# Attention to a context of 77 tokens: f16 pairs, a column of ones and a six-step order

## The reference

```python
q = split_heads(queries @ Wq + bq)          # 2 x 16 x 1024 x 16
k = split_heads(keys @ Wk + bk)             # 2 x 16 x 77 x 16, from ctx_1024
v = split_heads(values @ Wv + bv)
scores = jnp.einsum('bhqd,bhkd->bhqk', q, k) / jnp.sqrt(jnp.float32(HD))
scores = jnp.where(mask, -1e15, scores)     # layer 2
# layer 3: scores + attn_bias (2 x 16 x 1024 x 77), then where(mask == 0, -inf, scores)
attn = jax.nn.softmax(scores, axis=-1)
out = (attn @ v, heads side by side) @ Wo + bo
```

## Time and profile before

| what | value |
|---|---|
| runs, us | 3884.24, 3891.68, 3892.88 (median 3891.68) |
| profiled execution, us | 3897.72 |
| its span in the trace, us | 3896.1 |
| mean granted TensorE clock | 0.871 of 2.4 GHz |
| instructions | 66000 |
| block `c2a` in the trace | 2391.7 to 2544.0 us |
| block `c3a` in the trace | 3371.5 to 3526.8 us |

### The profile page before, as it was taken

How to read it: one execution, slowest core, us unless ns; L and a number is a source line. 1 busy time by engine, 2 the same in 40 slices (tenths; PEclk the granted TensorE clock), 3 DMA queues, 4 the chain that set the end, 5 groups by cost and what they waited for, 6 DMA issues and landing times. The chain is left out here.

```text
span 3896.1 us, 66000 instructions
## 1 busy us (share of the span) xinstructions
PE 3167.6 (81%) x24836; PEld 2157.7 (55%) x24837; DVE 2087.9 (54%) x3105; ACT 1832.3 (47%) x2854; POOL 1173.6 (30%) x851
## 2 busy tenths in 40 slices
PE   4979995816879998889994986968999999794495
PEld 2756664304436665346663654854666666583364
DVE  2968885493568763567853224635444444363122
ACT  2448883341348882358861112425555565242131
POOL 1239994000027880058761011210000000151102
PEclk7669997957889998989996996968999999796698
DMA  2421110000012210022216011001100000235211
GB/s 66 164 75 55 55 52 30 33 0 12 0 41 58 54 35 2 0 60 50 58 20 231 32 34 32 14 26 36 31 23 23 23 23 1 56 87 191 61 34 59
DMA packets 234091, 188.66 MB, mean 48 GB/s; under 512 B 136179, under 2 KB 193823, under 8 KB 233311
## 3 DMA queue, kind: packets, MB, share of 16 engines
q1 hardware_dynamic: 228542, 170.50, 15.5%
q0 software_dynamic: 5280, 14.42, 1.1%
HBM read 107.75 MB, written 35.59 MB: 37 GB/s over the span
## 5 line engine op out<-in xcount | busy, mean ns | idle before, releaser
L2212 POOL TENSOR_TENSOR lta_p_lo<-lta_p,lta_p_hi 128x1024 f16<-128x1024 f32 x256 | 539.1, 2133 | 527.4 <-DVE lta_p_hi L2335 527.4
L2407 ACT ACTIVATE lta_p<-lta_banks,lt_gmax 128x512 f32<-128x512 f32 x512 | 324.2, 683 | 113.1 <-PE lta_banks L2250 108.7
L3333 PE MATMUL m2e_h_ps<-m2e_x,m2e_w 128*128 128x512 f16 x1536 | 354.0, 381 | 22.5 <-DVE m2e_w L3438 19.0
L2318 DVE TENSOR_REDUCE lta_s_ps<-lta_s_ps 128x1 f32<-128x1101 f32 x240 | 314.2, 1309 | 106.8 <-PE lta_s_ps L2229 106.8
L3345 PE MATMUL m2e_y_ps<-m2e_w,m2e_hT 128*128 128x256 f16 x3072 | 355.6, 273 | 0.0
L3443 DVE TENSOR_TENSOR m2e_hT<-m2e_h,m2e_hT 128x512 f16<-128x512 f32 x256 | 177.3, 692 | 300.1 <-ACT m2e_hT L3386 298.5
L3345 PEld LDWEIGHTS m2e_y_ps<-m2e_w,m2e_hT 128*128 128x128 f16 x3072 | 300.5, 98 | 61.5 <-issue 0.5
L3386 ACT ACTIVATE m2e_h<-m2e_h_ps,m2e_h_bias,m2e_h_scale 128x512 f32<-128x512 f32 x256 | 199.5, 779 | 281.9 <-PE m2e_h_ps L3333 258.8
L985 POOL TENSOR_TENSOR c0a_tri_p_lo<-c0a_tri_p,c0a_tri_p_hi 128x1024 f16<-128x1024 f32 (+2 forms) x192 | 285.7, 1522 | 61.5 <-DVE c0a_tri_p_hi L1158 60.7
L3333 PEld LDWEIGHTS m2e_h_ps<-m2e_x,m2e_w 128*128 128x128 f16 x1536 | 150.6, 98 | 180.1 <-DVE m2e_w L3438 19.7
L1229 ACT ACTIVATE c0a_tri_p<-c0a_banks,c_size 128x512 f32<-128x512 f32 (+3 forms) x384 | 208.5, 577 | 45.2 <-PE c0a_banks L1053 33.8
(11 more groups left out here) (694 smaller groups left out, 6780.2 us busy)
## 6 DMA issues: line engine op xcount, KB each, us to landing
m_w<-in_L_ffn_w_dram SPq DMA_DIRECT2D x4, 8192.0 KB, 42.8
m_raw<-in_L_ffn_W_dram SPq DMA_DIRECT2D x16, 1024.0 KB, 6.6
lta_q<-ltb_qT SPq DMA_DIRECT2D x96, 128.0 KB, 2.4
c3a_bias<-in_fside_Bx16xSxS_dram SPq DMA_DIRECT2D x16, 616.0 KB, 4.7
c0a_tri_q<-c_near SPq DMA_DIRECT2D x96, 96.0 KB
c0a_tri_k<-c_mixed SPq DMA_DIRECT2D x96, 96.0 KB
lta_k<-ltb_kT SPq DMA_DIRECT2D x64, 137.6 KB, 2.5
lt_vh<-ltb_v SPq DMA_DIRECT2D x64, 128.0 KB
```

The source lines that it names most:

```text
L2212: nc.gpsimd.tensor_tensor(p_lo[:, slot, :], p32[:, p32_slot(h, j), :], p_hi[:, slot, :], ALU.subtract).then_inc(rested, 1)
L2318: nc.vector.tensor_reduce(ntop_of(h)[:, n:n + 1], scores(h, n), AX_X, ALU.max, negate=True).then_inc(top_ready, 1)
L2407: nc.scalar.activation(p32[0:rows, slot, c * 512:(c + 1) * 512], t_ps[0:rows, c, :], ACT.Exp, bias=bias, scale=p["gmax"][0:rows, 0:1]).the ...
L3333: last = nc.tensor.matmul(h_ps[:, f % RING, :], w1[:, v, a, c, f * P:(f + 1) * P], x16[:, b, c, n * CHUNK:(n + 1) * CHUNK], start=c == 0 a ...
```

## The change

`cross_attend` is rewritten.

- **f16 pairs.** DVE rounds the exponentials to f16 (`high`, by a maximum over an axis of one element, `halve`); POOL subtracts to get the rest (`low`, `rest`). PE turns both, 32 transposes per tile in f16, into three PSUM banks of 1024 f16 columns; ACT copies 4 x 1024 columns.
- **Values as f16 pairs with a column of ones.** `v16` holds per head 16 high columns, a one, and 16 low columns. A head takes three products, of 17, 16 and 17 columns, 48 per tile. The column of ones gives the sum, so the DVE sum (L3105) goes. `cross_operands` gets the scale of the values: a maximum (DVE), a reduction over partitions (POOL), six small DVE instructions.
- **Six steps.** The loops are written out in 21 steps. In step s, PE does scores of tile s, the transposes of tile s-3 between them, and the products of tile s-4; DVE the additions and maximum of tile s, the rounding of s-2 and the normalising (`level`) of s-5; POOL the shift of s-1 and the rest of s-2; ACT the exponential of s-2 and the copies of s-3. `z` has four buffers. PE waits per score bank, and reads `qT` directly; SP no longer copies the queries.
- **Side scores.** They come into three buffers, the first three tiles already during `cross_operands`. The mask is added on PE by a bf16 product with the identity (3 per tile in `c3`), and POOL's addition (L3029) goes.

```diff
         sp.dma_start(mask_in[:], mask.rearrange("b (t p) j -> p (b t) j", p=P)).then_inc(mask_loaded, 16)
+        if bias is not None:
+            for g in range(Side.RING):
+                bias.load(sp, g)
...
+        nc.gpsimd.partition_all_reduce(v_max[:], v_top[:], P, RMAX).then_inc(v_reduced, 1)
...
+        step(nc.vector.tensor_scalar(high, heads, v_size[0:NCTX, 0:1], None, ALU.mult))
+        step(nc.vector.scalar_tensor_tensor(low, heads, v_size[0:NCTX, 0:1], high, ALU.mult, ALU.subtract))
...
     @block.gpsimd
...
+        for s in range(STEPS):
+            if within(s - 1):
+                shift(s - 1)
+            if within(s - 2):
+                rest(s - 2)
...
     @block.tensor
...
+        def score(g, k):
+            if g:
+                pe.wait_ge(added, 3 * (g - 1) + k + 1)
...
+            if bias is not None:
+                last = nc.tensor.matmul(by_head(s_ps[:, k, 0:len(heads) * NCTX], len(heads)), ident_b[:],
+                                        spread(neg[:, g:g + 1, :], [P, len(heads), NCTX]), start=False, stop=True)
...
+        def turn(g, part, i):
+
+            n = 4 * g + 2 * part + i
+            if part == 0:
+                pe.wait_ge(halved, g + 1)
+            else:
+                pe.wait_ge(rested, g + 1)
+            if n >= PT:
+                pe.wait_ge(evacuated, n - PT + 1)
+            src = (high, low)[part][:, g % HALVES, :]
+            for r in range(H // 2):
+                h = i * (H // 2) + r
+                last = nc.tensor.transpose(pt_ps[0:NCTX, n % PT, r * P:(r + 1) * P], src[:, h * NCTX:(h + 1) * NCTX], ident_h[:])
+            last.then_inc(turned, 1)
+
+        def weigh(g):
+            u, b = g % OUT, g // TPB
+            pe.wait_ge(evacuated, 4 * g + 4)
+            if g >= OUT:
+                pe.wait_ge(normed, g - OUT + 1)
+            for h in range(H):
+                for part, a, width in ((0, 0, VW), (0, VW, HD), (1, 0, VW)):
+                    last = nc.tensor.matmul(o_ps[:, u, h * VW:h * VW + width], pT[0:NCTX, g % TURNED, part, h * P:(h + 1) * P],
+                                            v16[0:NCTX, b, h, a:a + width], start=h == 0 and part == 0 and a == 0,
+                                            stop=h == H - 1 and part == 1)
+            last.then_inc(weighed, 1)
...
     @block.vector
...
-            nc.vector.tensor_reduce(total[:, u, :], by_head(z[:, u, :]), AX_X, ALU.add).then_inc(summed, 1)
...
+            nc.vector.tensor_reduce(high[:, u, :], z[:, g % ROWS, :].unsqueeze(2), AX_X, ALU.max).then_inc(halved, 1)
...
+            nc.vector.reciprocal(inv[:, u, :], weights[:, :, HD]).then_inc(inv_ready, 1)
...
+            nc.vector.scalar_tensor_tensor(by_head(out[:, g, :]), weights[:, :, 0:HD], v_back[:, 0:1],
+                                           spread(inv[:, u, :].unsqueeze(2), [P, H, HD]), ALU.mult, ALU.mult).then_inc(normed, 1)
...
     @block.scalar
...
+        for s in range(STEPS):
+            if within(s - 2):
+                soften(s - 2)
+            if within(s - 3):
+                for part in range(2):
+                    for i in range(2):
+                        evacuate(s - 3, part, i)
```

More of the change, by code:

```diff
@@ L2974, in cross_attend @@
+        step(nc.vector.scalar_tensor_tensor(low, heads, v_size[0:NCTX, 0:1], high, ALU.mult, ALU.subtract))
+def cross_attend(nc, env, st, ctx, bias, qT, kbd, v16, v_back, neg, out):
     sb, ps, sem = st.sb, st.ps, st.sem
     half = H // DC
[L2976 to L2987, removed]
+    ROWS, HALVES, TOPS_KEPT, TURNED, PT, OUT = 4, 3, 3, 2, 3, 2
@@ L2988, in cross_attend @@
+    turned, evacuated, weighed, inv_ready, normed, table_loaded, filled = (
+        sem(n) for n in ("turned", "evacuated", "weighed", "inv_ready", "normed", "table_loaded", "filled"))
     block = ctx.enter_context(nc.Block())
     by_head = lambda ap, n=H: ap.rearrange("p (h j) -> p h j", h=n)
[L2990 to L3022, removed]
+    within = lambda g: 0 <= g < TILES
@@ L3024, in _ @@
+    STEPS = TILES + 5
+    if bias is not None:
+        @block.sync
+        def _(sp):
+            for g in range(Side.RING, TILES):
+                sp.wait_ge(added, 3 * (g - Side.RING + 1))
+                bias.load(sp, g)
     @block.gpsimd
     def _(pool):
[L3026 to L3029, removed]
@@ L3063, in weigh @@
[L3063 to L3077, removed]
-                                                   z[:, u, (4 * k + r) * NCTX:(4 * k + r + 1) * NCTX], env.ident[:])
-                        if r == 3:
-                            last.then_inc(p_turned, 1)
-                    if k >= 2:
-                        product(4 * (k - 2) + r)
@@ L3114, in _, with add @@
-        dve.sem_inc(z_added, AHEAD)
-        dve.sem_inc(normed, AHEAD)
-        tiles(dve, attend, normalise)
-        dve.wait_ge(normed, TILES + AHEAD)
+        def add(g, k):
+            heads = BANK_HEADS[k]
+            n, cols = len(heads), slice(heads[0] * NCTX, (heads[-1] + 1) * NCTX)
+            dve.wait_ge(scored, 3 * g + k + 1)
+            if g >= ROWS:
+                dve.wait_ge(rested, g - ROWS + 1)
+            if bias is not None:
+                bias.wait(dve, g)
+                other = by_head(bias.tiles[:, g % Side.RING, cols], n)
+            else:
+                other = spread(neg[:, g:g + 1, :], [P, n, NCTX])
+            nc.vector.tensor_tensor(by_head(z[:, g % ROWS, cols], n), by_head(s_ps[:, k, 0:n * NCTX], n), other, ALU.add).then_inc(added, 1)
@@ L3119, in _ @@
+        for s in range(STEPS):
+            if within(s):
+                add(s, 0)
+            if within(s - 2):
+                halve(s - 2)
+            if within(s):
+                add(s, 1)
+                add(s, 2)
+            if within(s - 5):
+                level(s - 5)
+            if within(s):
+                largest(s)
+        dve.wait_ge(normed, TILES)
     @block.scalar
     def _(act):
-        nc.scalar.activation(total[:, 0, :], env.ones[:, 0:H], ACT.Exp).then_inc(table_loaded, 1)
+        nc.scalar.activation(inv[:, 0, :], env.ones[:, 0:H], ACT.Exp).then_inc(table_loaded, 1)
```

165 lines of the change are left out of this document (100 added, 65 removed).

## The result

The changed kernel takes 3788.7 us (median of 4 runs, 3783.0 to 3791.1), the kernel before, beside it, 3892.3 (3884.2 to 3902.4). The ratio is 0.973, 95% interval [0.9705, 0.9756]: 103.6 us less. Five further rounds gave 3788.5 us and 0.9733 [0.972, 0.9747]. In the profiled executions the span falls from 3896.1 to 3789.5 us.

What follows compares the result with a forecast made beforehand. PE was taken to bound both attention blocks. Start, eleven full steps and end gave 100.9 us against 152.3 and 108.0 against 155.3, so 98.7 us less: 3891.7 - 98.7 = 3793.0 us, range 3780 to 3832.

Steps and rivals of the forecast that it cites:

- What bounds it: Both attention blocks before the change: PE fills them, busy 142.3 of 152.3 us and 142.4 of 155.3 us.
- PE's step: PE per tile: scores 2.3, transposes 1.84, products 1.2, sum 5.35 us in place of 7.58; 5.9 us with the second block's mask.
- Rival 2: PE's small products cost more than 0.025 us: at 0.058, 3831 us, chance 0.09; at 0.116, 3898 us, chance 0.01.
- the far end of rival 2: PE's products at the f32 price of 0.116 us each: 105 us more, no gain, 3898 us; chance 0.01.
- the allowance: Full steps: waits among four near-equal engines not all hidden, so 5.6 and 6.15 us instead of 5.35 and 5.9.
- an extra 0.25 us on DVE: DVE's step: 0.25 us added because the additions wait each for themselves, giving 5.3 us.
- Start and end: Both blocks' edges: start 22 us, 23 in the second with bf16 products; end 17.3 us, a chain over ACT and POOL.
- The clock: PE in the full steps: stays at 2.4 GHz, since products stand alone for only 1.2 us a step.
- Edits at nothing: Direct queries, value scales, side scores, written-out code: counted as free; scales uncovered would cost 7 us per block, code below 1.
- Rival 4: Scale of the values or first side scores end behind the queries: at most 7 us a block, 3807 us; chance 0.04.
- Size against the medians: Whole kernel: the 98.7 us gain came from a profiled execution 6.0 us above the median, but was subtracted from the median.

Runs made afterwards that it cites:

- Experiment 1: Changed kernel's six-step order kept, but f32 transposes and one f32 product of 17 columns per head, no rounding or rest: 3884.4 us, before beside it 3890.9.
- experiment 3: Changed kernel with all 48 products of a tile issued twice, then three times: 3831.5 us and 3886.9 us.
- Experiment 8: Changed kernel with two PSUM buffers for the transposes in place of three: 3794.7 us.
- experiment 6: Two versions of the changed kernel moving copies, shifts and rests at block ends to DVE, PE waiting later for identities: 3785.8 us (both ends), 3787.0 us (tail only).
- experiment 2: Changed kernel's f16 pairs and column of ones kept, but each engine works in the old order, tile s then s-1: 4095.2 us.
- experiment 4: Changed kernel without the products with the low half of the values, 16 of 48 per tile: 3774.8 us.
- `shared_tail`: Changed kernel, but DVE takes tile 15's shift and rest and every second copy of tiles 13 to 15; PE's early identity wait dropped: 3787.0 us, 0.9723.

## Why the prediction held, step by step

The forecast was 3793.0 us, 3780 to 3832; measured were 3788.7. Its two blocks, with start (to the end of the first tile's products), eleven steps and end, in us:

| | forecast, first | measured | forecast, second | measured |
|---|---|---|---|---|
| start | 22 | 24.4 | 23 | 22.1 |
| eleven steps | 61.6 | 58.0 | 67.7 | 63.9 |
| end | 17.3 | 16.5 | 17.3 | 15.8 |
| block | 100.9 | 98.9 | 108.0 | 101.8 |

- **What bounds it.** Right: PE filled the block and set the time. Experiment 1 shows it from one side (no waits left on PE, hardly anything gained), experiment 3 from the other (1.21 us of PE work added, 1.21 us more a step).
- **PE's step.** The sum of 5.35 us measured 5.27, that of 5.9 measured 5.81. The term on which most hung, 0.025 us a product taken over from another attention, was 0.0254. Rival 2 falls with it. The transposes, 0.0575 in the row, were 0.056. The f32 prices of 0.116 and 0.13 us were too high, since they were read from durations up to the end of the last instruction: from start to start they are 0.107 (1.93 us for 18 products) and 0.109 (the transposes of experiment 1). The forecast does not use them, only the far end of rival 2 and the 8.0 us expected in experiment 1 do. The Trainium skill ("TensorE: Matmul & The Clock Gate", LDWEIGHTS) would have a load of 77 columns take 64 ns, an estimate by its formula; here transposes of that form follow each other in 56, loads included, so as with the 97 columns the trace does not agree.
- **The step that failed: the allowance.** "With four engines within 10% of each other waits will not all be hidden; I take 5.6 and 6.15 us a step." PE waited for nobody. 0.33 or 0.34 us in each of 22 steps is the 7.4 us by which the eleven steps of both blocks came out shorter, nearly all of the 8.2 by which the blocks did. DVE and ACT were taken at 5.3 us and POOL at 4.9, and measured 4.95, 4.99 and 4.83 (50.76, 51.11 and 49.45 us of 54.00, times 5.27). I had added durations, and neighbouring instructions overlap by some 0.1 us: the rounding from 2444.64 takes 1.44 us and the next addition starts at 2445.99, three copies of 1.01 us take 2.94 in a row. Nor was there an extra 0.25 us on DVE for additions that wait each for themselves. Experiment 8 shows how near the allowance lay: one buffer less, and the step is the 5.60 that I had.
- **Start and end.** The first start was 2.4 us longer than forecast, the second 0.9 shorter; the ends were 0.8 and 1.5 shorter. Two things in the first start are not in the forecast: the half clock from 2405 to 2411, and POOL, which began its first shift 1.85 us after the maximum was there (2398.32 to 2400.17). The row puts the idle time down to "issue", that is, to nothing that the profile shows, so its cause stays open:

```profile
2396.88 1.44 DVE L3146 TENSOR_REDUCE c2a_top<-c2a_z 128x16 f32<-128x1232 f32 x1
...
2400.17 4.45 POOL L3052 TENSOR_TENSOR c2a_z<-c2a_z,c2a_top 128x1232 f32<-128x1232 f32 x2 [7.18 <-issue]
```

- **The clock.** Right: 1.00 in all full steps. It was argued from what stands in a row on PE, and experiments 1 and 3 fit that: in their full steps it fell behind rows of 3.5 or 3.6 us of narrow products, of f32 or of f16 (behind every second or third of them in the first block), while PEclk stayed at 1.00 with the 1.2 us of the changed kernel and the 2.4 us of the products made twice. The Trainium skill (same page, Part 4) says of transposes that they do not count as PE being busy in the same way. The full steps can't decide that, since a third of each is transposes (32 x 0.056 = 1.79 of 5.27 us) and the rest is not; the rows of before, in which only transposes stand ahead of the rise, are what does not agree with it.
- **Edits at nothing.** The scales of the values took 4.0 us from the values (3305.54) to the last of their instructions (3309.54), not 7; the last query copy ends at 3317.5. Rival 4 falls. The queries read directly are not at nothing at the blocks' starts, as the prediction says too: the first scores start 0.6 us into each block, where they started 2.3 and 2.4 us into it before, behind a wait for the copy. What the written-out code costs was not measured by itself.
- **Size against the medians.** The blocks gained 106.9 us and the medians 103.6. The profiled execution of before lay 5.4 us above its median, that of the change 2.5, which is 3 of the difference.

## What to carry to other kernels

Price a rewrite of a saturated engine by rows of the same form and type elsewhere in the same trace, and count gaps between starts, not durations. Splitting one f32 product into f16 pairs makes three products of each here and still cuts their time from 3.5 us a tile (experiment 1) to 1.2, but it lengthens the chain from scores to products by two steps on other engines: alone it cost 204 us, and only with enough tiles under way did it gain. When waits are gone from the full steps, what is left at a block's start and end hangs on the clock and on other engines' late starts as well as on the order, so shortening one wait there may buy nothing.

## What the runs showed of the hardware beyond that

- PE's clock falls while PE is busy all the time: PEclk 0.79 and 0.64 (experiment 1) and a mean of 0.89 (experiment 3, three times) with 60.00 of 60.00 us busy, each time behind 3.5 or 3.6 us of products of 16 or 17 columns, though not behind every such row.
- A wait of 1.9 us on PE was followed by 3 us at half clock (experiment 6), and waits of 3.4, 1.5 and 1.2 us a tile by a mean of 0.61 (experiment 2).
- With four engines at 99% or more (experiment 4) POOL's shift takes 2.25 us, DVE's reductions 1.43 and ACT's exponential 1.24. In the kernel before, where DVE was busy half of the time and ACT and POOL less, they took 2.25, 1.43 and 1.23.
- POOL's first shift in a block began 0.3 us (second block of the changed kernel) to 3.9 us (first block of `shared_tail`) after the maximum it waits for, 0.1 in the first block before; what decides it is not shown.
